# Keys produced transposed: the key maximum taken along the free axis, and the exponentials turned back on TensorE

## The reference, cut to what matters

```
q = x @ Wq.T + bq; k = x @ Wk.T + bk; v = x @ Wv.T + bv     # 16 heads of 16 channels
q = softmax(q, axis=-1)
k = softmax(k, axis=-2)                                       # over the 1024 tokens of the batch
state = einsum('bhnd,bhne->bhde', k, v)
out = einsum('bhnd,bhde->bhne', q, state)
x = layernorm(x + (layernorm(out)*ln_g + ln_b) @ Wo.T + bo)
```

## Time and profile before

| | |
|---|---|
| runs | 1242.4, 1242.64, 1237.84 us, median 1242.4 |
| profiled execution | 1242.11 us, of which the span from the first to the last instruction is 1240.4 us |
| busy share of the span | PE 87%, PEld 73%, DVE 60%, ACT 43%, POOL 52% |
| mean granted TensorE clock | 0.938 |
| steps 0 to 37 (keys, chain stages, weights) | up to 398.4 us of the span |
| mixed steps and experts | from 398.4 us |

### The profile page before, as it was taken

How to read it: one execution, slowest core, us unless ns; L and a number is a source line. 1 busy time by engine, 2 the same in 40 slices (tenths; PEclk the granted TensorE clock), 3 DMA queues, 4 the chain that set the end, 5 groups by cost and what they waited for, 6 DMA issues and landing times.

```text
span 1240.4 us, 27263 instructions
## 1 busy us (share of the span) xinstructions
PE 1080.2 (87%) x8576; PEld 910.7 (73%) x8576; DVE 742.2 (60%) x1813; ACT 528.0 (43%) x1148; POOL 641.0 (52%) x739
## 2 busy tenths in 40 slices
PE   6668898798864998989989999999999999999960
PEld 3345676576644887878878888888888888888750
DVE  2568988888875665765674544444444444444326
ACT  2765665544543445554433333333333333333214
POOL 3003332657665566766777555555555555554324
PEclk9878998998876998999999999999999999999985
DMA  4553222213022323334344544655444445553336
GB/s 126 167 163 96 84 81 80 51 44 84 27 63 57 81 46 67 62 66 83 47 81 74 88 78 78 78 79 78 78 79 78 75 75 75 76 75 58 63 55 247
DMA packets 159969, 100.63 MB, mean 81 GB/s; under 512 B 106956, under 2 KB 151168, under 8 KB 159840
## 3 DMA queue, kind: packets, MB, share of 16 engines
q1 hardware_dynamic: 129824, 63.21, 20.1%
q0 software_dynamic: 30016, 35.68, 19.3%
HBM read 49.55 MB, written 31.59 MB: 65 GB/s over the span
## 4 chain that ended last, share of the span: by engine, by line
PE 67%; DVE 12%; ACT 8%; issue 4%; DMA 4%; POOL 4%; SPq 1%; DVEq 0%; ACTq 0%; POOLq 0%
PE big L1801 28%; PE big L1820 15%; PE trans L1820 11%; PE big L1838 2%; POOL slot_records L851 2%; ACT pr L992 1%; PE big L1730 1%; PE small L1709 1%; PE trans L1632 1%; PE small L1741 1%; PE small L1887 1%; DMA w_down<-in_L_ffn_down_w_dram 1%; DVE stat L1130 1%; PE big L1840 1%; ACT L992 1%
## 5 line engine op out<-in xcount | busy, mean ns | idle before, releaser
L1801 PE MATMUL big<-xgT,w_up 128*128 128x256 f16 (+1 forms) x3456 | 410.7, 268 | 10.7 <-ACT h L976 6.2
L976 ACT ACTIVATE h<-big,up_scale 128x512 f32<-128x512 f32 x270 | 185.6, 687 | 438.0 <-PE big L1801 429.2
L1801 PEld LDWEIGHTS big<-xgT,w_up 128*128 x3456 | 326.3, 99 | 54.3 <-issue 14.3
L881 POOL DMA_INDIRECT token_sums<-y,rec x135 | 223.4, 1654 | 246.6 <-ACT y L984 216.8
L1404 DVE TENSOR_SCALAR hh<-h,h_scale 128x512 f16<-128x512 f32 x270 | 133.1, 493 | 346.7 <-ACT h L976 346.1
L1820 PE MATMUL big<-w_down,hh 128*128 x1312 | 223.7, 272 | 2.5 <-DVE hl L1406 2.2
L1406 DVE SCALAR_TENSOR_TENSOR hl<-h,h_scale,hh 128x512 f16<-128x512 f32 x270 | 203.3, 753 | 9.7
L1820 PE MATMUL big<-w_down,hl 128*128 x656 | 178.8, 273 | 0.0
L866 POOL DMA_INDIRECT xg<-token_rows,rec x135 | 136.5, 1011 | 51.3 <-issue 39.0
L851 POOL DMA_INDIRECT slot_records<-recs,posi x128 | 133.2, 1040 | 34.8 <-issue 34.8
L1820 PE MATMUL trans<-w_down,hh 128*128 x848 | 144.6, 273 | 2.3 <-DVE hl L1406 2.3
(11 more groups left out here) (261 smaller groups left out, 1416.1 us busy)
## 6 DMA issues: line engine op xcount, KB each, us to landing
w_down<-in_L_ffn_up_w_dram SPq DMA_DIRECT2D x8, 1024.0 KB, 5.0
w_down<-in_L_ffn_down_w_dram SPq DMA_DIRECT2D x7, 1024.0 KB, 5.7
wqkv_XA<-in_x_dram SPq DMA_DIRECT2D x32, 128.0 KB, 2.7
XRES<-in_x_dram SPq DMA_DIRECT2D x32, 128.0 KB
token_sums<-X SPq DMA_DIRECT2D x32, 128.0 KB, 1.7
token_rows<-XR SPq DMA_DIRECT2D x32, 128.0 KB, 1.7
sums<-token_sums SPq DMA_DIRECT2D x8, 512.0 KB, 6.5
out_dram<-sums SPq DMA_DIRECT2D x8, 512.0 KB, 2.6
```

What stands on the lines that cost most here:

```text
L881: pool.indirect_dma_start(acc[0:EARLY_BATCHES * N, :] if t < EARLY else acc, bass.IndirectOffsetOnAxis(ap=rec[:, t % RING, j, 0:1], axis=0 ...
L976: act.activation(h[:, i % H_RING, :], psu[up_bank(i)], ACT.Gelu_apprx_tanh, scale=k["up_scale"][:, t:t + 1]).then_inc(gelu_ready, 1)
L1801: ins = pe.matmul(psu[up_bank(i)][:, j * size(t):(j + 1) * size(t)], w[:, ws, c, m:m + P], xgT[:, t % 2, xs * CC + c, 0:size(t)], start=(n ...
```

## The change

K is produced with the channels on the partitions and the tokens along the row. With that:

- PE: the product of K and V with 512 columns becomes four products of 128 columns for K (weights stationary, x moving) and two of 256 columns for V. The two transposes of the running maximum and the product with ones go. In the step after the closing step PE turns the 16 exponentiated 128x128 blocks back, two tiles (4 blocks) to a PSUM bank, two banks ahead of the probability transposes and two after the context logits.
- DVE: the running maximum (8 a batch), the reduction of the turned maximum, the diagonal, the two rounding instructions and the 5 subtractions go. In their place stand 5 row reductions of the keys (groups of 1, 1, 3, 2 and 1 tiles; four of them in `take_qkv`, each of which now waits for the copy of K and of V of its last tile; one in the closing step), a reduction over the 5 parts, an addition and a subtraction of 128x2 elements.
- ACT: the 5 exponentials become 10 (each group for each channel half), with the negative maximum as a bias read from a column. Five copies bring the turned exponentials back (two for the first pair of tiles, one for each other pair).
- SP: bk is loaded as a column (128x2) and not spread over all partitions.
- K's tile in SBUF gets another order of its axes; its size is the same.

```diff
@@ bank_uses
-        if closing(s) is not None:
-            use(sm, "km", closing(s))
...
+        if state_built(s) is not None:
+            for q in range(KEY_PAIRS // 2):
+                use(tr, "e", state_built(s), q)
         if c3 is not None:
             use(tr, "pa", c3)
             use(tr, "pb", c3)
-        if closing(s) is not None:
-            use(sm, "kb", closing(s))
         if c2 is not None:
             use(big, "lg", c2)
+        if state_built(s) is not None:
+            for q in range(KEY_PAIRS // 2, KEY_PAIRS):
+                use(tr, "e", state_built(s), q)
@@ ACT
+            def copy_keys(b, q):
+                act.wait_ge(tr_ready, TR["e", b, q] + 1)
+                src = tr_bank(("e", b, q))[:, :, :].rearrange("p (i c) k -> p i c k", i=2)
+                if q == 0:
+                    act.activation(key_tile(TB * b), src[:, 0], ACT.Copy)
+                    act.activation(key_tile(TB * b + 1), src[:, 1], ACT.Copy).then_inc(tr_copied, 1)
+                else:
+                    act.activation(K[:, :, 2 * q:2 * q + 2, :].rearrange("p c i k -> p i c k"), src, ACT.Copy).then_inc(tr_copied, 1)
...
+                last = state_built(s)
+                if last is not None:
+                    for q in range(KEY_PAIRS // 2):
+                        copy_keys(last, q)
                 if c3 is not None:
                     copy_probs("pa", c3)
                     copy_probs("pb", c3)
+                if last is not None:
+                    for q in range(KEY_PAIRS // 2, KEY_PAIRS):
+                        copy_keys(last, q)
...
-                    for q in range(len(KEY_GROUPS)):
-                        act.wait_ge(ks_ready, len(KEY_GROUPS) * b + q + 1)
-                        act.activation(key_group(b, q), key_group(b, q), ACT.Exp).then_inc(ke_ready, 1)
+                    act.wait_ge(kshift_ready, b + 1)
+                    for i0, i1 in KEY_GROUPS:
+                        for c in range(CC):
+                            keys = key_group(b, i0, i1, c)
+                            act.activation(keys, keys, ACT.Exp, bias=kshift[:, c:c + 1]).then_inc(ke_ready, 1)
@@ DVE, take_qkv
-                dve.wait_ge(kv_ready, 2 * g + 1)
-                if i == 0:
-                    dve.tensor_copy(kmx[:, :], key_tile(g)).then_inc(kmx_ready, 1)
-                else:
-                    dve.wait_ge(kmx_ready, g)
-                    dve.tensor_tensor(kmx[:, :], kmx[:, :], key_tile(g), ALU.max).then_inc(kmx_ready, 1)
+                for q, (i0, i1) in enumerate(MAX_GROUPS):
+                    if i1 == i + 1 and i1 < TB:
+                        part_maximum(g // TB, q)
...
+            def part_maximum(b, q):
+                i0, i1 = MAX_GROUPS[q]
+                dve.wait_ge(kv_ready, 2 * (TB * b + i1))
+                keys = key_tile(TB * b + i0) if i1 == i0 + 1 else K[:, :, i0:i1, :].rearrange("p c i k -> p c (i k)")
+                dve.tensor_reduce(kpart[:, q, :], keys, AX_X, ALU.max).then_inc(kpart_ready, 1)
@@ DVE, key_maximum (shift_keys is gone)
+                part_maximum(b, len(MAX_GROUPS) - 1)
+                dve.wait_ge(kpart_ready, len(MAX_GROUPS) * (b + 1))
+                dve.tensor_reduce(kmax[:, :], kpart[:, :, :].rearrange("p q c -> p c q"), AX_X, ALU.max).then_inc(kmax_step, 1)
+                dve.wait_ge(kmax_step, 2 * b + 1)
+                dve.tensor_tensor(kmax[:, :], kmax[:, :], bk_col[:, :], ALU.add).then_inc(kmax_step, 1)
+                dve.wait_ge(kmax_step, 2 * b + 2)
+                dve.tensor_tensor(kshift[:, :], bk_col[:, :], kmax[:, :], ALU.subtract).then_inc(kshift_ready, 1)
@@ PE
+            def turn_keys(b, q):
+                dst = turn_into(("e", b, q))
+                for i in range(2):
+                    group = next(n for n, (i0, i1) in enumerate(KEY_GROUPS) if i0 <= 2 * q + i < i1)
+                    pe.wait_ge(ke_ready, CC * (len(KEY_GROUPS) * b + group + 1))
+                    for c in range(CC):
+                        ins = pe.transpose(dst[:, CC * i + c, :], key_tile(TB * b + 2 * q + i)[:, c, :], ident[:, :])
+                ins.then_inc(tr_ready, 1)
...
+                    for o in range(CC):
+                        for c in range(CC):
+                            pe.matmul(dst[:, o * P:(o + 1) * P], wqkv[:, c, C + o * P:C + (o + 1) * P], xT[:, c, :], start=(c == 0), stop=(c == CC - 1))
                     for c in range(CC):
-                        pe.matmul(dst[:, 0:2 * C], xT[:, c, :], wqkv[:, c, C:3 * C], start=(c == 0), stop=(c == CC - 1))
+                        pe.matmul(dst[:, C:2 * C], xT[:, c, :], wqkv[:, c, 2 * C:3 * C], start=(c == 0), stop=(c == CC - 1))
```

82 lines of the change are left out of this document (32 added, 50 removed).

## The result

In 19 runs of each kernel on one chip the changed kernel took 1245.58 us (median; 1241.32 to 1248.64), the kernel before 1239.16 (1233.37 to 1244.42): a ratio of 1.0048 with a 95% interval of 1.0034 to 1.0062, 6.4 us slower. I had forecast 1247.7, or 5.6 more than the profiled execution of before. The profiled execution of the changed kernel took 1245.45 us; that of before, 1242.11, lies 3 us above its own median of 19, so the two traces differ by only 3.3 us.

What follows compares the result with a forecast made beforehand. Before the experts no engine is full; the chain of waits to their start at 398.43 us bounds the kernel. Terms 3.1 + 2.4 + 0.7 + 0.2 + 0.4 - 1.2 = +5.6 us on 1242.1 give 1247.7, range 1239 to 1255.

Steps and rivals of the forecast that it cites:

- the gain on DVE ends at ACT: Step 17: DVE done 3.7 us earlier, but exponentials wait for x2T and take 3.6 us; `pr` starts at 161.2 as before.
- the ladder: Steps 18 and 27: PE's turns and ACT's copies alternate before the state; in step 18 it starts at 169.6, not 167.21.
- My term for batch 1: Steps 17 and 18: state starts later by +2.4 us, from 0 if the copies hide to +4.
- For batch 2 the term: Steps 26 and 27: +2.4 us as in batch 1, less 1.1 of DVE work and 0.6 of PE: +0.7, from -2 to +3.
- The K product: K in 8 PE instructions: +0.06 us a tile, on the path in perhaps a third of tiles, +0.4 in all (0 to 1.9).
- batch 0: Steps 8 and 9: exponentials +1.4, copies +2.1, waiting 0.5, less 0.9 slack; `split_high` 3.1 us later (+1.4 to +5.5).
- in every state step DVE waits for PE's state: Steps 9, 18 and 27: PE's state ends the step, and DVE and ACT wait for it; no size given.
- The sums nearly cancel: Ordinary steps: maxima and waits removed against row reductions and V waits added; -0.4 us for each of batches 1 to 3.
- the signs I had listed: Step 18: DVE idle over 6 us, state 8.4 us after `pr`; step 9: `split_high` 3 us later; experts at about 404.
- the rival of no effect: Whole kernel: DVE's lead from step 17 catches up the later state; +1 us, 1243; chance 0.12.
- the faster one: Closing steps: DVE stays the bound and ACT fits in, batches 1 and 2 gain 3.9 and 4.4; -10, 1232; chance 0.11.
- the slower one: Step 9's state wholly at low clock, +2.0, and ACT's instructions not overlapping, +1.5 for each of three batches; +12, 1254; chance 0.27.

Runs made afterwards that it cites:

- the other K product: Kernel before with K made by four products of 128 columns, weights standing, as in the change: 1239.11 against 1239.66 us, ratio 0.9995.
- the direct shift: Kernel before with the spread maximum subtracted from the keys straight out of PSUM, without the two K bias instructions: 1236.39 against 1237.90 us, ratio 0.9983.
- the third experiment: Changed kernel with five plain exponentials a batch, without bias, in place of ten with; turning back stays: 1241.53 against 1239.27 us for the kernel before.
- the second experiment: Changed kernel without the transposes of the exponentials and their copies back: 1240.38 against 1239.27 us for the kernel before, ratio 1.0010.

## Why the prediction was right, and where it was not

The time, its sign and its size came out (1245.6 for 1247.7; +6.4 for +5.6). Its main mechanism did too: the way back through PE and ACT and the ten exponentials cost more than DVE's relief brings. That the sum came so close is in part luck. For the closing and state steps of batches 0 to 2 I had +6.2 and the traces give 4.05 + 1.3 + 0.2 = 5.6. For the ordinary steps of batches 1 and 2 I had -0.8 and they give +2.3. And the last stretch gives back 5.1 us for which there was no term.

**Right in the main: the gain on DVE ends at ACT.** I had the exponentials of step 17 hang on x2T and last 3.6 us, so that `pr` starts where it did. The order came out: `pr` follows x2T and ten exponentials. From the first exponential to `pr` it is 3.8 us, zT's copy of 0.27 among it. Counted from state 0, `pr` starts 76.2 and 75.2 us later before and 76.4 and 76.1 after. But the ordinary steps, which grew, lie in that count. Counted from tile 15's Q bias it is 18.8 and 19.9 us before and 18.1 in both traces after, and from tile 23's 20.75 before and 19.4 and 19.1 after. So 0.7 to 1.8 of the 3.9 and 4.4 us did get past ACT, with x2T, which comes earlier. The kernel before without the subtraction agrees from the other side: DVE's relief is worth 2.2 us there by the medians, and hardly more than 4.

**Right: the ladder.** From `pr` to the state 8.4 us were worked out, 8.66 came; 6.0 were there before, and without turning back it is 5.8. My term for batch 1 was +2.4; steps 17 and 18 grew by 1.3 in the mean, as `pr` came earlier, and the rest of the stretch's 3.1 is in the ordinary steps. For batch 2 the term was +0.7 and steps 26 and 27 grew by 0.2; that the whole stretch grew by 0.7 doesn't prove the parts. The K product was priced at +0.4 (0.06 us in a third of the tiles would be 0.6) and no cost was seen.

**Mis-sized: batch 0.** The term was +3.1, the traces give +3.7 and +4.4. The exponentials account for 1.4 of it, as priced. Behind them I took the copies on ACT for the path and the transposes for hidden but for 0.5 us. The path to the landmark was that one: in all four traces the reciprocal follows `split_low` on DVE, which follows `split_high`, and starts 4.4 us after `split_high` does. After the change DVE shows it so:

```profile
86.77 2.35 DVE L1150 SCALAR_TENSOR_TENSOR w_up<-w_down,wsc,w_up 128x2048 f16<-128x2048 f32 x1 [4.82 <-ACT w_up L979]
```

The item of the sum that was too small is the wait for the transposes. ACT's copies waited 0.82 + 0.20 + 0.41 + 0.26 = 1.7 us for them in the first trace, where the 16 transposes ran at 1.2 GHz in one piece of 3.67 us, and 1.0 in the second, where the first of them still ran at 2.4 GHz. Counted from the first exponential, `split_high` started 4.4 and 3.7 us later than before (10.6 and 9.9 for 6.2 us), and not 3.1. A second path is about as long: the transposes and, behind them, the state on PE, which ended 0.9 and 1.2 us before the reciprocal started; the chain that ended last goes through it. The prediction's sentence that in every state step DVE waits for PE's state doesn't hold for step 9, before or after. The clock in step 9 of the changed kernel (stretch, PE, PEld, DVE, ACT and POOL busy, clock, DMA share, GB/s):

```profile
80.00:82.00 2.00, 2.00 (x10) 1.70 (x11) 1.45 (x7) 0.99 (x4) 0.00 (x0) 0.50 1.06 362
82.00:84.00 2.00, 2.00 (x10) 1.92 (x11) 0.00 (x0) 1.31 (x3) 0.00 (x0) 0.50 0.09 25
84.00:86.00 2.00, 2.00 (x15) 2.00 (x14) 0.00 (x0) 2.00 (x3) 0.00 (x0) 0.70 0.00 0
```

The clock is at its lower level from before PE starts (PE had no work from 76.0 to 79.6) until the state is some 1.4 us under way. This looks as the rule of the Trainium skill says (TensorE: Matmul & The Clock Gate, Part 4: PE-mode transpose: transposes do not count as busy in the way products do). But the runs speak against it. In the kernel with plain exponentials PE had the same two small products (78.82) and 16 transposes first (timeline of PE):

```profile
79.06 3.59 PE L1767 MATMUL trans<-ident,K 128*128 128x128 f32 x16
82.44 3.77 PE L1909 MATMUL small<-V,K 128*128 128x129 f32 x31
```

and its clock there (stretch, PE busy, clock, DMA share, GB/s):

```profile
82.25:82.50 0.25, 0.25 (x3) 0.50 1.04 344
...
82.75:83.00 0.25, 0.25 (x4) 1.00 0.43 123
```

There the clock is back at 2.4 GHz at about 82.75 us, 0.3 us into the state, with hardly anything but transposes behind it; that the transposes brought it back is not shown by that. And in the kernel without turning back, where PE goes into the state with no transpose at all, the state takes 5.92 us with the clock at 0.50 from about 79.4, when PE was idle, until 86.0, 4.8 us after PE's start. How long the clock stays down in step 9 does not go with the presence of transposes. It differs between two traces of one kernel (the changed kernel's second has a clock of 1.00 at PE's start, 80.2 us, and the lower level only from 81.1 to 84.5), and what else decides it is open.

**Wrong: "The sums nearly cancel: -0.4 for each of batches 1 to 3".** The ordinary steps of batches 1 and 2 came out longer, not shorter. I had compared busy times and let the longer wait for V stand in one clause. In the trace the removed maxima were 11.4 us busy and 5.5 idle; the new reductions are 11.4 busy (4.1, 3.8, 2.7 and 0.8, the closing steps' among them) and 11.0 idle (3.8, 2.5, 1.1 and 3.6). Most of the new idle time, 5.3 us, stands in the state steps 9, 18 and 27 (3.05, 1.81 and 0.48), where the first tile's reduction waits for ACT's copy of V. In the ordinary steps of batches 1 to 3 the idle time is 4.2 us for 3.9 before, so there it is not the total that changed but where it falls. In step 13 the new reduction waits 1.89 us and takes 0.95, 2.84 together where the running maximum had 1.61 and 0.43; PE's idle time behind it is 2.69 us and not 1.90. The steps without a reduction became shorter (the one of tile 11 from 7.2 and 6.8 to 6.6), those with one longer (tile 12 from 12.1 and 10.6 to 12.9 and 13.0, tile 14 from 9.5 and 11.0 to 11.6). Both traces after have a low clock in both of the longer steps, where each trace of before has it in one, so how much of the growth is the reduction and how much the clock isn't separated. The experiment without the running maximum shows that what stands at this place in DVE's list can be worth some 8 us, as much as all that the change moves in the closing steps. I looked at the closing steps because the chain's long rows stand there; the ordinary steps are 28 times a short row.

**Not foreseen: what is given back.** From state 2 to the experts the changed kernel is 4.6 to 5.5 us shorter. 3.6 of it are between state 2 and tile 31 (67.5 before, 64.0 and 63.8 after), and there a low stretch of the clock is missing. Before and after, the same time of the span:

```profile
288.00:292.00 4.00, 4.00 (x13) 2.91 (x13) 2.21 (x8) 0.77 (x2) 3.42 (x4) 0.50 0.18 45
292.00:296.00 4.00, 4.00 (x17) 2.76 (x16) 0.93 (x3) 1.06 (x4) 2.76 (x4) 0.75 0.23 43
```

```profile
288.00:292.00 4.00, 2.78 (x18) 2.10 (x16) 3.76 (x15) 1.06 (x5) 3.25 (x7) 1.00 0.72 247
292.00:296.00 4.00, 2.79 (x21) 2.44 (x22) 3.38 (x10) 1.79 (x6) 3.04 (x8) 1.00 0.12 39
```

Summed over half-microsecond stretches, both traces of before have 13.7 us of low clock between state 2 and tile 31 and both of after 3.4. It isn't owed to any one part of the change: the kernels before with ten exponentials and with the other K product have 3.4 too, and take 63.9 and 64.0 us there, and so does the changed kernel with plain exponentials (64.1); the one with the direct shift has 13.7 and takes 67.6. The other changed kernels and the one without the subtraction lie between, with 6.5 to 10.2 us of low clock and 65.6 to 66.5 us. Only the kernel without the running maximum stands apart, 63.9 us with 10.2 us of low clock. What decides how much of this work meets the low clock is not shown; shifts of a few us in earlier steps are my guess. While it is open, sums over single waits can't give the time to better than the 3.6 us that hang on it.

**Of the signs I had listed**, four came: ten exponentials of about 3.6 us with `pr` behind them; the longer way from `pr` to the state; `split_high` later without idle time before it; experts of unchanged length (1.05 us more, within the scatter). Two did not. DVE's idle time before the reciprocal of the state in step 18 is 2.5 us (2.7 before), not over 6: what DVE gained it spends in earlier waits of that step (1.1 for Q's product, 1.8 at L1188 for V's copy, 2.5 for ACT's XR). And the experts start at 400.5, not 404: batch 0 costs more, the clock gives back more.

The change of 0.48% lies at the 0.5% that I had named as what a measurement can tell from no change. With 19 runs of each it could tell more: the interval, 0.34 to 0.62%, leaves out zero, and with it the rival of no effect (+1 us), the faster one (-10) and the slower one in its full size (+12).

## What to carry to other kernels

An engine's total busy time says little where each engine runs a fixed list: the place of an instruction that waits is what costs. Ask of every wait what stands behind it; here 28 maxima of 0.42 us, one of which waits 1.6 us for a copy and holds back Z and PE, were worth 7.7 us together, and the subtractions, 3 batches of about 4 us, only some 2 by the medians, because another engine was next. When work is moved from one engine to another for a better layout, count the way back with its banks and round trips before the gain. Exponentials with a bias from a column should be as long as the layout allows: merging ten into four took the way from the first one to `pr` from 3.8 to 2.7 us.

A version that beats both kernels was among the runs: shifting by the maximum of a batch's first tile, 8 us shorter. The softmax does not change under any shift common to all tokens, but the guard against overflow becomes weaker, since later keys may lie above that maximum. Whether the full maximum could be had for nearly the same time by placing it behind Z in DVE's list was not tried.

## What the runs showed of the hardware

In step 9 TensorE's granted clock fell to 1.2 GHz around or after an idle time of PE (76.0 to 79.6 us in the changed kernel, 76.9 to 78.6 before); in the second trace of before PE was idle from 73.9 to 75.9 us and the clock stayed at its full level up to 84 us, through the whole state. Between state 2 and tile 31 traces with 13.7 us of low clock took 67.5 to 67.6 us and those with 3.4 us 63.8 to 64.1. The clock came back (0.50 to 1.00 at 82.75 us in the third experiment) with 16 transposes of 128x128 float32 and only two small products behind it, 3.9 us after PE had begun; in step 9 of the first trace of before, with products alone, it was some 3.6 us, and in the second experiment 4.8. A DVE subtraction that reads its second operand from PSUM took 0.40 us for 256 columns in step 17, as the one from SBUF (0.42).
